# Two-layer gated FFN on one core: the z48 product ahead of the f16 product in each slot, the low half of transposed h ahead of the copy of c, last slots and routing transposes elsewhere in TensorE's order

## The reference

```python
# layer 0: c is a gelu MLP over the channels, with a time mask; then an int4 product in fp16
h = gelu(einsum('bct,bch->bht', x * cmask, W_sess[session]) + b_sess[session])
c = (einsum('bht,hs->bst', h, W2) + b2) * tmask
x = x + (c.astype(f16) @ dequantize(qweight, qzeros, scales) + bias)
# layer 1: base product with a LoRA by batch entry, then a product with experts
u = x @ base_weight.T + base_bias + (x @ A[adapter].T) @ Bw[adapter].T
H = u @ W.T + b ;  z = u @ A
logits = 0.5 * H[:, 1::2, :8] / max|H..| + 0.5 * delta / max|delta|   # delta = z[:, 1::2] @ LiMEs.T
w = softmax(logits) * sigmoid((softmax(logits) - second_largest) / 0.5), normalised
x = x + H + ((z * (w @ LiMEs)) @ Bmat) * scaling
```

## Time and profile before

| | us |
|---|---|
| runs of the kernel | 228.84, 227.46, 225.64 (median 227.46) |
| the profiled execution, its own device time | 227.16 |
| its span in the trace | 225.4 |
| TensorE matmul busy | 194.6 (86%) |
| VectorE busy | 132.5 (59%) |
| ScalarE busy | 65.3 (29%) |
| GpSimd busy | 60.9 (27%) |

### The profile page before, as it was taken

One profiled execution on the slowest core, in us unless ns is written; L12 is line 12 of the kernel. 1 busy time (PEld: TensorE's weight loads), 2 busy tenths in 40 slices (PEclk: granted clock), 3 DMA queues, 4 the chain that ended last, 5 costly groups with the idle time before them and its releaser, 6 DMA issues.

```text
span 225.4 us, 3201 instructions
## 1 busy us (share of the span) xinstructions
PE 194.6 (86%) x962; PEld 129.7 (58%) x962; DVE 132.5 (59%) x323; ACT 65.3 (29%) x129; POOL 60.9 (27%) x91
## 2 busy tenths in 40 slices
PE   2649998998796799999999999999986899899994
PEld 0628875556464456455564555654545768588882
DVE  4498559893446444666657467564754178640871
ACT  0360064341323114344243443334412020013000
POOL 4450003004300405422544144241016623221000
PEclk9995899999699679999999999999999999999999
DMA  5999100973891012312422141114213773524794
GB/s 165 313 252 321 25 0 5 226 287 93 233 360 52 13 52 48 125 52 64 135 56 54 45 157 52 49 46 132 60 47 107 232 246 102 180 93 154 269 347 164
DMA packets 25473, 30.50 MB, mean 135 GB/s; under 512 B 7536, under 2 KB 16624, under 8 KB 25456
## 3 DMA queue, kind: packets, MB, share of 16 engines
q1 hardware_dynamic: 21656, 20.25, 29.2%
q0 software_dynamic: 3328, 9.96, 13.9%
q10 hardware_dynamic: 472, 0.09, 0.2%
HBM read 19.54 MB, written 6.55 MB: 116 GB/s over the span
## 4 chain that ended last, share of the span: by engine, by line
PE 66%; DVE 17%; issue 7%; ACT 5%; DMA 2%; POOL 1%; POOLq 0%; ACTq 0%; DVEq 0%
PE ps L1041 14%; PE ps L965 8%; PE ps L989 7%; PE ps L900 6%; PE ps L1016 5%; PE ps L926 4%; ACT xT_all L389 4%; PE ps L999 3%; PE ps L1014 3%; DVE cT L709 2%; PE ps L1045 2%; DMA WT<-L_dram,idx_l 2%; PE ps L941 2%; DVE mask L518 2%; PE ps L1174 1%
## 5 line engine op out<-in xcount | busy, mean ns | idle before, releaser
L1041 PE MATMUL ps<-G,xT_all 128*128 128x512 f32 x168 | 48.8, 417 | 0.0
L340 POOL DMA_INDIRECT lz<-L_z_dram,idx_l x16 | 15.8, 985 | 87.3 <-PE ps L1028 73.3
L1041 PEld LDWEIGHTS ps<-G,xT_all 128*128 128x128 f32 x168 | 29.6, 191 | 16.3 <-issue 11.8
L514 DVE TENSOR_TENSOR xT_all<-ps,xT_all 128x512 fp32r<-128x512 f32 (+2 forms) x37 | 18.9, 512 | 22.9 <-ACT xT_all L389 22.4
L389 ACT ACTIVATE xT_all<-ps 128x512 fp32r<-128x512 f32 (+1 forms) x36 | 14.7, 453 | 50.0 <-PE ps L999 36.1
L431 ACT ACTIVATE gel<-ps,bsess 128x512 f32<-128x512 f32 x32 | 20.2, 683 | 16.4 <-PE ps L953 16.4
L349 POOL DMA_INDIRECT WT<-L_dram,idx_l x16 | 15.3, 959 | 23.2 <-PE ps L1045 18.6
L989 PE MATMUL ps<-W,cT 128*128 128x512 f16 x64 | 16.6, 382 | 5.1 <-DVE cT L709 3.7
L1016 PE MATMUL ps<-az,xT_all 128*128 128x256 f32 x64 | 15.5, 325 | 5.4 <-DVE zall L514 5.4
L514 DVE TENSOR_TENSOR x_all<-x_all,ps 128x512 f32<-128x512 f32 x21 | 13.5, 684 | 10.3 <-PE ps L1174 10.0
L965 PE MATMUL ps<-gel,W2bd 128*64 128x512 f32 x64 | 18.2, 647 | 1.6 <-ACT gel L431 1.6
(11 more groups left out here) (188 smaller groups left out, 284.4 us busy)
## 6 DMA issues: line engine op xcount, KB each, us to landing
az<-AT SPq DMA_DIRECT2D x64, 64.0 KB
out<-x_all SPq DMA_DIRECT2D x16, 256.0 KB, 2.9
x_all<-in_x SPq DMA_DIRECT2D x3, 1024.0 KB, 9.2
L_dram<-xT_all SPq DMA_DIRECT2D x4, 512.0 KB, 8.5
x_all<-in_L_ffn_W SPq DMA_DIRECT2D x2, 512.0 KB, 4.3
x_all<-in_L_cond_base_weight SPq DMA_DIRECT2D x2, 512.0 KB, 6.9
x_all<-in_L_cond_lora_B_w SPq DMA_DIRECT2D x4, 256.0 KB, 7.1
x_all<-in_x SPq DMA_DIRECT2D x2, 512.0 KB, 6.4
```

The source lines that it names most:

```text
L340: nc.gpsimd.indirect_dma_start(lz[:, t % 2, :].bitcast(F32), None, L_z_dram, bass.IndirectOffsetOnAxis(idx_l[:, t:t + 1], 0)).then_inc(s_l ...
L514: return nc.vector.tensor_tensor(o, a, bb_, op)
L1041: mm(dst, xT_all[:, t, a * KC + j, :], G[:, c, j, :], start=i == 0, stop=False, skip_group_check=True)
```

## The change

Four edits, no instruction added or taken away in number:

1. TensorE's slots: `h_to_z(n-3)` stands ahead of `ffn(n-1)` instead of behind it.
2. VectorE: the end of a turn is `x_lo`, `hT_lo`, `cT_copy`, `time_mask` instead of `x_lo`, `time_mask`, `cT_copy`, `hT_lo`.
3. Last slots: TensorE does `h_to_z(13)` and four matmuls of `main(4)` ahead of `ffn(15)`, and the last five of `main(4)`, the LoRA rows among them, ahead of `x1_transposes(15)`. `gather_L(4)` goes out in turn 15 of GpSimd's loop instead of turn 16.
4. Routing: the third product stands behind all of `main(9)` and two matmuls of `main(10)` (before: behind 12 of the 14 of `main(9)`), and the fourth four matmuls later (before: two). The wait on `s_f16` moves with the first matmul of `main(10)`.

```diff
-                if n >= 4 and n % 3 == 1 and n // 3 <= NI:
+                if n >= 4 and n % 3 == 1 and n // 3 < NI:
                     gather_L(n // 3 - 1)
+                if n == NT - 1:
+                    gather_L(NI - 1)
...
                 if n - 1 < NT:
                     x_lo(n - 1)
+                if 2 <= n < NT + 2:
+                    hT_lo(n - 2)
+                if n < NT:
+                    cT_copy(n)
                 if n + 1 < NT:
                     time_mask(n + 1)
-                if n < NT:
-                    cT_copy(n)
-                if 2 <= n < NT + 2:
-                    hT_lo(n - 2)
...
                 hidden(n)
+                h_to_z(n - 3)
                 ffn(n - 1)
-                h_to_z(n - 3)
                 h_and_z(n - 2)
...
+            h_to_z(NT - 3)
+            main(4, 5, 4)
             ffn(NT - 1)
-            h_to_z(NT - 3)
             h_and_z(NT - 2)
-            main(4, 5, 7)
+            main(4, 9, 5)
             x1_transposes(NT - 1)
             h_transpose(NT - 2)
-            main(4, 12, 2)
...
-            main(9, 0, 12)
+            main(9, 0, 14)
+            pe.wait_ge(s_f16, NT)
+            main(10, 0, 2)
             pe.wait_ge(s_rv, R_W)
             nc.tensor.transpose(ps[6][:, 0:P], rt[:, 2, :], ident[:, :]).then_inc(s_rp, 1)
-            main(9, 12, 2)
+            main(10, 2, 4)
             pe.wait_ge(s_rv, R_WT)
             mm(ps[6][:, :], rt[:, 5, :], BD, start=True, stop=True).then_inc(s_rp, 1)
-            pe.wait_ge(s_f16, NT)
-            main(10, 0, 14)
+            main(10, 6, 8)
```

## The result

The kernel after took 215.09 us (median of four runs, 213.33 to 216.54) beside 226.59 us before (median of four, 225.64 to 228.84). The ratio, taken over the faster executions of each kernel alone, those within 1.5% of its fastest, is 0.945, 95% interval 0.932 to 0.959. The forecast was 218.2 us with a range of 214.8 to 221.4. The direction was right and the size too small: 0.945 times the 226.59 of before is 214.2, just under the range, and the median itself lies 0.3 us inside it. The profiled execution after took 216.5 us, its span is 214.7.

The account below looks back on a forecast made before the run. TensorE was taken to set the pace, busy 6.59 of 7.09 us in a slot. Gains of 5.4 (slots), 2.45 (last slots) and 1.1 (routing), say 9.0 us, off 227.16 gave 218.2 us, range 214.8 to 221.4.

Parts of the forecast that it names:

- The slots: Steady-stage slots: covering the wait for `add_z` wins 0.55 us a slot, 0.1 with `add_main`; 5.4 us over 13 slots.
- A delay of 0.15 us for `ffn`: Slot start: the later copy of c and two products ahead delay `ffn` by 0.15 us, bounds 0.07 and 0.30.
- the chain of 1.26 us: Slots with `add_main`: VectorE's mask, `add_main`, `add_z` and 0.16 to be seen, from the copy's end; taken as 1.32 from `ffn`.
- The last slots: Behind the loop: the 2.82 us wait for tile 4's LoRA rows goes, new waits appear; gain 2.45 us, bounds 1.9 and 2.8.
- The LoRA rows of tile 5: Last slots: these gathered rows land at 176.7 and are needed at 177.8; half a us late gives the lower bound 1.9.
- The routing: Routing products: 0.83 us of wait for `R_W` and a 0.25 us gap are covered by matmuls; gain 1.1 us (0.6 to 1.1).
- The sum: Whole kernel: 5.4 + 2.45 + 1.1, say 9.0 us, off the profiled execution's 227.16 gives 218.2 us, bounds 216.4 and 221.1.
- The clock stays full in slot 3: Rival, slot 3: shorter idle time keeps the clock full, 3.4 us more won, 214.8 us; chance 0.12.
- No gain in the slots: Rival, slots: `hT_lo` and two products cost as much ahead of `ffn` as the ring behind it; 223.6 us; chance 0.13.
- the slot's head waits: Rival, slot start: `h_to_z` holds TensorE's queue until `hT_lo`; slower, 232.5 us at 1.1 us beyond the cover; chance 0.04.

Follow-up runs that it names:

- edit 4: Against the kernel before, only the routing transposes moved later in TensorE's order; 224.56 us at the median of ten executions, ratio 0.998.
- edit 1 alone: Against the kernel before, only `h_to_z` put ahead of `ffn` in TensorE's slots, VectorE's order kept; one execution took 223.25 us.
- edit 3: Against the kernel before, only the last slots reordered, with `gather_L(4)` one turn earlier; 223.78 us at the median, ratio 0.988.
- edits 1 and 2: Against the kernel before, TensorE's slots and VectorE's end of a turn reordered, last slots and routing kept; 219.15 us at the median, ratio 0.966.
- edit 2 alone: Against the kernel before, only VectorE's order at the end of a turn changed, TensorE's kept; one execution took 232.97 us.

## Why the prediction fell short

**The slots, right.** A delay of 0.15 us for `ffn` was taken; the copy was 0.19 later in its chain. `h_to_z` had its operand in time: 0.13 us lie between the end of the subtraction and its start. A slot won 0.56 to 0.59 us against 0.55, one with `add_main` 0.18 to 0.21 against 0.1. The second difference is a slip in the prediction: the chain of 1.26 us counts from the end of the copy, and `ffn` starts 0.06 after that end, so from the start of `ffn` it is 1.20 and not 1.32. With 1.20 the gain is 0.22, and the trace has 1.18 (95.35 to 96.53). The wait for `add_z` in those slots was forecast at 0.3 to 0.4 and is 0.15. Together slots 4 to 14 won 0.5 us more than forecast.

**The last slots, right.** 0.8 us at `h_to_z(14)` were forecast, 0.69 came; `x1_transposes(15)` was late by 0.16 at most against 0.3. The LoRA rows of tile 5 came in time.

**The routing, right in the product.** 1.1 us forecast, 1.05 in the stage table, 1.2 alone.

**The base and the clock, wrong.** The step that failed is the one ahead of the rivals, *The sum*: 9.0 us of work were taken off the profiled execution's own 227.16 us, so that the clock which this execution happened to have stayed in the forecast as a fixed part, and the change's own effect on the clock stood at nothing. What the runs show in its place: that execution lost 8.6 us to the clock, before loses 7.6 on average and after 5.3. So 1.0 of the miss is the choice of one execution as a base, and 2.3 is what after loses less than before, by the means over 8 and 20 executions. The other way go 0.4, by which that execution's product lies under the mean of before. With 217.2 - 9.1 + 5.3 and the 1.76 around the span the time is 215.2, and the eight executions took 215.1 on average. All terms of that sum are measured, so it is no second proof; it shows which term of the prediction was off. The work was not: 9.1 by the product, 9.0 by the prediction.

That the work agrees to 0.1 us is in part luck. Slots 4 to 14 won 0.5 more than forecast and slot 3 0.15 less, and of the profiled pair the stages show 9.4 of work, where the product shows 9.0.

The clock was no fixed part of 227.16 that a shorter program takes along. It is a loss behind the long idle times of TensorE, not in every execution, and the change takes one such place away (the 2.8 us for the LoRA rows). It also shortens another (slot 3, 2.75 to 2.49 us), but that this made the fall there smaller is not shown: the profiled pair lost 3.4 and 1.7 us at slot 3, and the trace of edit 4, with the old 2.75, shows the same 0.94 as after.

**The rival on the clock, right in kind, mis-sized.** "The clock stays full in slot 3" had a chance of 0.12 and all of 3.4 us. In the profiled execution after, the clock still fell there, with half of that loss. The sentence beside it was the error: that the 2.82 us lowered nothing in one trace was read as if they never did, so their removal was priced at the gap alone. The four other traces with this gap all show the fall behind it. The prediction also cited the Trainium skill, "TensorE: Matmul & The Clock Gate", section "What's actually happening", that the point of change varies from run to run. The runs agree in kind: the same program before lost 5.1 us to the clock in six executions of 20, and 10.2 or 10.3 in five.

**The other rivals.** "No gain in the slots" and "the slot's head waits" are refuted by the windows of slot 7. Edit 1 without edit 2 shows what the second would look like: 0.44 us of wait at the head of a slot. The prediction had 0.3 us won in a slot for that case, and 0.2 came.

What stays open: how the clock's mean gain of 2.3 us divides between the gap that was removed, slot 3, and chance in the set-up. The table's means don't say: edit 3, without the gap, loses 7.1, edits 1 and 2, with it, 6.2, and edit 4, which changes neither place, 6.9, so that such a mean moves by 0.7 without a cause that is known. The ten traces show where the clock fell, but too few of each kernel to say how often. Why it fell for longer in some traces than in others behind the same idle time is not known either.

## What to carry to other kernels

Where two engines hand a small result to and fro, look for the work that is ready anyway and put it between the product and the wait for its sum. The other engine's order has to change with it, or the head of the queue waits instead: edit 1 alone won 2.6 us, edit 2 alone lost 2.0, both together 5.1 and with the last slots in order more. Where TensorE has idle times like the 2.5 to 3.1 us here, compare span times granted clock, not times, and take the mean over several executions. Price the removal of such a gap with a part of the clock's loss behind it, even if the one trace at hand shows none, and take the base of a forecast from several executions and not from the profiled one.

## What the runs showed of the hardware

The span at full clock is steadier than the time: over 20 executions of before the product of span and clock lies within 216.4 and 218.1, while the times go from 223.9 to 230.1. The clock's losses come in levels, in before 5.1 (six times), 6.7 to 6.9 (four), 8.6 to 8.8 (five) and 10.2 to 10.3 (five). The same gap of 2.8 to 3.0 us behind the loop left the clock full in one trace (before) and put TensorE at its half level in four (edit 1, edit 2, both, edit 4). An idle time of 2.5 to 3.1 us at slot 3 did so in eight traces of eight, one of 0.35 us in none of two. So an edit that wins 1.2 us by the product, as edit 4 did, may show as 0.2% in ten executions beside 13.
